# Slot tables of a routed MLP: single-pass products, shares behind the indices, bounds read in portions, a router on raw rows

## The reference, cut to what matters

```python
x = x + _L1_xattn_ref(_layernorm(x), ctx, ctx)      # gelu(xn @ ctx.T) @ ctx
xn = _layernorm(x)
logits = xn @ w_router                               # 8 experts
probs = softmax(logits); sel = argmax(probs); wgt = probs[sel]
for e in range(8):
    h = relu(xn @ w1[e] + b1[e]);  y = h @ w2[e] + b2[e]
    out = out + ((sel == e) * wgt)[:, None] * y
x = x + out
```

## Time and profile before

| | |
|---|---|
| median of 3 runs | 681.23 us (680.93 to 682.4) |
| the profiled execution: time | 682.95 us |
| its span | 681.0 us |
| TensorE busy | 583.7 us (86%) |
| VectorE busy | 494.2 us (73%) |
| ScalarE busy | 315.0 us (46%) |
| GpSimd busy | 271.3 us (40%) |
| `context_mlp`, from its first VectorE instruction to the meeting | 425.9 to 504.2 us |
| `experts` | 504.2 us to the end |

### The profile page before, as it was taken

One profiled execution on the slowest core, in us unless ns is written; L12 is line 12 of the kernel. 1 busy time (PEld: TensorE's weight loads), 2 busy tenths in 40 slices (PEclk: granted clock), 3 DMA queues, 4 the chain that ended last, 5 costly groups with the idle time before them and its releaser, 6 DMA issues. The chain is left out here.

```text
span 681.0 us, 11778 instructions
## 1 busy us (share of the span) xinstructions
PE 583.7 (86%) x3680; PEld 510.6 (75%) x3680; DVE 494.2 (73%) x961; ACT 315.0 (46%) x570; POOL 271.3 (40%) x270
## 2 busy tenths in 40 slices
PE   4489999995899999999999987678539799989983
PEld 3478988884688888888888876447528799879873
DVE  4799999984139888888988967476525866885682
ACT  1135545543258778778788850333101513442240
POOL 3434444660024344344354422032035652682341
PEclk9789999997899999999999999775558999989988
DMA  7122421100522322332232000814033441691100
GB/s 232 31 78 78 107 81 31 32 1 1 135 48 47 88 52 49 72 68 48 56 85 48 1 1 0 325 63 127 37 100 140 138 148 31 209 336 42 39 19 2
DMA packets 24123, 54.89 MB, mean 81 GB/s; under 512 B 4857, under 2 KB 9722, under 8 KB 22025
## 3 DMA queue, kind: packets, MB, share of 16 engines
q1 hardware_dynamic: 20328, 46.69, 23.2%
q0 software_dynamic: 2256, 5.54, 3.0%
q10 hardware_dynamic: 1488, 2.05, 1.0%
HBM read 33.27 MB, written 4.87 MB: 56 GB/s over the span
## 5 line engine op out<-in xcount | busy, mean ns | idle before, releaser
L939 POOL TENSOR_SCALAR h_p<-h_p,h_rs 128x1024 f32<-128x1024 f32 x64 | 72.2, 1128 | 116.3 <-DVE h_rs L1042 116.2
L1049 DVE TENSOR_REDUCE h_nmx<-h_psS 128x1 f32<-128x1024 f32 x64 | 78.2, 1221 | 28.7 <-PE h_psS L1141 27.4
L1029 DVE TENSOR_TENSOR h_pTl<-h_psT,h_pTh 128x512 fp32r<-128x512 f32 x128 | 81.6, 679 | 4.4 <-ACT h_pTh L969 4.4
L969 ACT CAST h_pTh<-h_psT 128x512 fp32r<-128x512 f32 x128 | 69.2, 590 | 31.3 <-PE h_psT L1099 31.2
L996 ACT ACTIVATE h_p<-h_psS,h_nmx 128x1024 f32<-128x1024 f32 x64 | 72.2, 1129 | 14.1 <-DVE h_nmx L1049 14.1
L1110 PE MATMUL h_psO<-h_pTh,h_vs 128*128 128x256 f32 x256 | 70.0, 306 | 3.0 <-DVE h_oT L1037 2.3
L1099 PE MATMUL h_psT<-ident,h_p 128*128 128x128 f32 x512 | 67.5, 273 | 1.4 <-DVE h_pTl L1029 1.2
L1099 PEld LDWEIGHTS h_psT<-ident,h_p 128*128 128x128 f32 x512 | 59.2, 140 | 11.2 <-issue 3.3
L341 POOL TENSOR_TENSOR a_p<-a_p,a_rs 128x616 f32<-128x616 f32 x32 | 39.0, 1219 | 62.8 <-DVE a_rs L445 62.7
L1110 PE MATMUL h_psO<-h_pTl,h_vs 128*128 128x256 f32 x256 | 63.6, 282 | 0.0
L1141 PE MATMUL h_psS<-h_kh,h_qs 128*128 128x512 f32 x128 | 55.7, 435 | 0.0
(11 more groups left out here) (295 smaller groups left out, 1498.5 us busy)
## 6 DMA issues: line engine op xcount, KB each, us to landing
wst<-in_m_w SPq DMA_DIRECT2D x16, 1024.0 KB, 5.8
bias<-in_m_b SPq DMA_DIRECT2D x8, 640.0 KB, 7.5
h_kh<-h_hi SPq DMA_DIRECT2D x30, 128.0 KB, 2.3
h_kl<-h_lo SPq DMA_DIRECT2D x30, 128.0 KB, 2.3
fw<-in_f_w SPq DMA_DIRECT2D x8, 384.0 KB, 4.1
rows<-x_all SPq DMA_DIRECT2D x4, 516.0 KB, 3.6
a_qs<-a_qhi SPq DMA_DIRECT2D x16, 128.0 KB, 2.3
a_qs<-a_qlo SPq DMA_DIRECT2D x16, 128.0 KB, 2.4
```

Source lines behind the costliest of these rows:

```text
L939: pool.tensor_scalar(pr[:, u % 4], pr[:, u % 4], rs[:, u:u + 1], 0.0, ALU.mult, ALU.add).then_inc(pn_ready, 1)
L969: act.copy(pTh[u // QP % 2][:, hf * HK:(hf + 1) * HK, u % QP * P:(u % QP + 1) * P], psT[hf][:]).then_inc(pT_hi, 1)
L1029: vec.tensor_tensor(pTl[u // QP % 2][part], psT[hf][:], pTh[u // QP % 2][part], ALU.subtract).then_inc(pT_lo, 1)
L1049: vec.tensor_reduce(nmx[:, u:u + 1], psS[u % 2][:], AX.X, ALU.max, negate=True).then_inc(max_ready, 1)
```

## The change: what it does

Four edits, all in `context_mlp` and `experts`.

- **Router on raw rows.** `normalise(NC + n)` is gone. TensorE transposes the rows of `x_all` as they are (waiting for `x_done`), and `route` multiplies them with `wrc`, the router's weights less their column means. The column sums come from a product with a matrix of ones (two products of 8 columns, placed behind `hidden(1)`), and VectorE makes `wrc` between `gelu(0)` and `normalise(2)`. The logits so lack the factor `rstd`, which VectorE multiplies into `e` after the subtraction of the largest.
- **Slots first, shares later.** `sent` has the token number alone, in fp32r, as `here` is; `inverse` is 16 products with 26 columns. The sum, the reciprocal, and a split of `wgt` in two parts, `whole` (fp32r) and `rest`, follow behind `here`. When `src` is written, VectorE makes `shared` (both parts, 52 columns), TensorE multiplies it with `here` (16 products), and VectorE adds the two results into `share`, last in the block.
- **Moved work.** The two `low_second` of expert 0 go from VectorE's stream in `context_mlp` to its `change(0)` in `experts`. The two `low_first` of expert 1 go from GpSimd's stream in `experts` to `context_mlp`, ahead of its wait for `src`. Gather 1 goes behind the meeting, and each tile is handed on three gathers later.
- **Bounds in portions.** The eight ends are read in portions of 2 to 4 between the first pieces of `change(0)` and `body(0, 0)`.

```diff
-        here = sb("c_here", [P, T, P])
-        sent = sb("c_sent", [P, T, 2, TG])
+        here = sb("c_here", [P, T, P], F32R)
+        sent, shared = sb("c_sent", [P, T, TG], F32R), sb("c_shared", [P, T, 2, TG], F32R)
+        whole, rest = sb("c_whole", [P, T], F32R), sb("c_rest", [P, T])
...
@@ gpsimd of context_mlp
             power(2)
             power(3)
+            for hf in range(2):
+                low_first(pool, t, 1, hf)
             pool.wait_ge(stored, 16 * NC)
             pool.wait_ge(src_ready, 1)
             gather(pool, t, 0)
-            gather(pool, t, 1)
...
@@ vector of context_mlp
             gelu(0)
+            vec.wait_ge(col_ps, 1)
+            vec.scalar_tensor_tensor(wrc[:], column.unsqueeze(1).to_broadcast([P, KD, NE]), -1.0 / D, wr[:], ALU.mult,
+                                     ALU.add).then_inc(wrc_ready, 1)
             normalise(2)
...
-                normalise(NC + n)
...
-            vec.tensor_tensor(e[:], psR[:], most, ALU.subtract).then_inc(shifted, 1)
+            link(vec.tensor_tensor(e[:], psR[:], most, ALU.subtract))
+            vec.wait_ge(rstd_ready, NC)
+            vec.tensor_tensor(e[:], e[:], rstd4.unsqueeze(2).to_broadcast(full), ALU.mult).then_inc(shifted, 1)
...
-            vec.wait_ge(exp_done, 1)
-            link(vec.tensor_reduce(tot[:], e[:], AX.X, ALU.add))
-            vec.reciprocal(wgt[:], tot[:])
...
-            for x, value in enumerate((tok1, wgt)):
-                ins = vec.tensor_tensor(sent[:, :, x], passed[:], value[:].unsqueeze(2).to_broadcast(wide), ALU.mult)
-            ins.then_inc(sent_ready, 1)
+            vec.tensor_tensor(sent[:], passed[:], tok1[:].unsqueeze(2).to_broadcast(wide), ALU.mult).then_inc(sent_ready, 1)
             for n in range(NC):
                 part, box = slice(n * CH, (n + 1) * CH), [P, CH, P]
                 vec.tensor_tensor(here[:, part], num[:].unsqueeze(1).to_broadcast(box),
                                   place[:, part].unsqueeze(2).to_broadcast(box), ALU.is_equal).then_inc(here_ready, 1)
-
-            for x in range(2):
-                low_second(vec, t, 0, x)
+            vec.wait_ge(exp_done, 1)
+            link(vec.tensor_reduce(tot[:], e[:], AX.X, ALU.add))
+            link(vec.reciprocal(wgt[:], tot[:]))
+            link(vec.tensor_copy(whole[:], wgt[:]))
+            link(vec.tensor_tensor(rest[:], wgt[:], whole[:].bitcast(F32), ALU.subtract))
 
             vec.wait_ge(inv_ps, 1)
...
+            vec.tensor_scalar(src[:], inverse, -1.0, 0.0, ALU.add, ALU.max).then_inc(src_ready, 1)
+            vec.tensor_tensor(shared[:, :, 0], passed[:], whole[:].bitcast(F32).unsqueeze(2).to_broadcast(wide), ALU.mult)
+            vec.tensor_tensor(shared[:, :, 1], passed[:], rest[:].unsqueeze(2).to_broadcast(wide),
+                              ALU.mult).then_inc(shared_ready, 1)
...
+            vec.wait_ge(share_ps, 1)
+            link(vec.tensor_copy(share[:], shares_in[:, 0]))
+            vec.tensor_tensor(share[:], share[:], shares_in[:, 1], ALU.add)
...
@@ tensor of context_mlp
+            pe.wait_ge(full_ready, 1)
+            for k in range(KD):
+                ins = pe.matmul(column, full_ones[:], wr[:, k], start=(k == 0), stop=(k == KD - 1))
+            ins.then_inc(col_ps, 1)
...
             ins.then_inc(inv_ps, 1)
+            pe.wait_ge(shared_ready, 1)
+            pe.wait_ge(dst_read, 1)
+            for i in range(T):
+                ins = pe.matmul(shares_in, here[:, i], shared[:, i], start=(i == 0), stop=(i == T - 1))
+            ins.then_inc(share_ps, 1)
...
@@ experts, tiles
-            ends = [load(eng, ENDS + e, MT - (NE - 1 - e), e + 2) for e in range(NE)]
-            change(0)
-            body(0, 0)
+            ends = []
+
+            def bounds(n):
+                for e in range(len(ends), len(ends) + n):
+                    ends.append(load(eng, ENDS + e, MT - (NE - 1 - e), e + 2))
+
+            change(0, bounds)
+            body(0, 0, bounds)
...
@@ gpsimd of experts
+            gather(pool, t, 1)
             gather(pool, t, 2)
-            arrived(pool, t, 0)
-            gather(pool, t, 3)
-            arrived(pool, t, 1)
-            gather(pool, t, 4)
-            arrived(pool, t, 2)
-            for hf in range(2):
-                low_first(pool, t, 1, hf)
-            for g in range(5, NG):
+            for g in range(3, NG):
+                arrived(pool, t, g - 3)
                 gather(pool, t, g)
-                arrived(pool, t, g - 2)
+            arrived(pool, t, NG - 3)
```

More of the change, by code:

```diff
@@ L1440, in transpose @@
             def transpose(i):
-                pe.wait_ge(xn_ready, i + 1)
+                n = i % NC
+                if i < NC:
+                    pe.wait_ge(xn_ready, i + 1)
+                else:
+                    pe.wait_ge(x_done, n + 1)
                 if i >= 1:
@@ L1615, in x_high, with change @@
                 act.copy(xh[:], psX[:]).then_inc(xh_ready, 1)
-            def change(e):
+            def change(e, bounds=None):
                 if e == 0:
@@ L1625, in change, with body @@
                         high_first(act, t, e + 1, hf)
-            def body(g, e):
+            def body(g, e, bounds=None):
+                if bounds:
+                    bounds(3)
                 x_high(g + 1)
+                if bounds:
+                    bounds(2)
                 for hf in range(2):
@@ L1657, in finish, with change @@
                                          ALU.add).then_inc(y_done, 1)
-            def change(e):
+            def change(e, bounds=None):
                 if e == 0:
+                    for x in range(2):
+                        low_second(vec, t, 0, x)
                     normalise(0)
@@ L1686, in body @@
                 normalise(g + 2)
+                if bounds:
+                    bounds(4)
             tiles(vec, change, body)
```

38 lines of the change are left out of this document (20 added, 18 removed).

## The result

| | before | changed |
|---|---|---|
| median | 681.15 us (680.93 to 682.4, 4 runs) | 672.56 us (667.16 to 673.38, 4 runs) |
| ratio, 95% interval | | 0.9855 [0.9824, 0.9885] |
| profiled execution: time, span | 682.95, 681.0 us | 673.38, 671.3 us |
| mean granted clock of that execution | 0.916 | 0.925 |

The change takes 8.6 us off the medians and 9.6 off the profiled executions. The forecast was a gain of 7.3 us and a median of 673.9.

A forecast was written before the change was run, and what follows sets the result against it. Four pieces in series were taken to bound the kernel: MLP's tail, slot stage, meeting, eight bound loads. 0.8 + 1.0 + 3.5 + 0.3 + 2.5 - 0.8 = 7.3 us gained gave 673.9 us, range 670.2 to 678.2.

The forecast's parts named there:

- (a): Router on raw rows, MLP's tail: earlier update and output product, less the column sums' delay; net 0.8 us gained.
- the 1.6 us that I named as the upper end: MLP's tail: extra gain if the earlier start kept or regained full clock for output product and transposes; not counted on.
- (b): Slot tables: sum, reciprocal and second multiply leave the chain ahead of the token product; 1.0 us gained.
- (c): Token product: 16 passes with 26 columns instead of 32 with 52, at 0.22 us each; 3.5 us gained.
- Rival 1: Narrow single passes run near the bf16 pace, so both slot products get shorter; 671.5 us, chance 0.16.
- (d): From `src` to the meeting: VectorE's wait for the shares replaces GpSimd's drain as last; 0.3 us gained.
- (e): Start of the experts: two `low_second` replace eight loads ahead of VectorE's first normalise; 2.5 us gained.
- (f): First tiles: remaining bound loads cost 0.3 us and a shifted clock rise 0.5; together 0.8 us lost.
- The experts are taken to shift as a whole: Behind the first tiles: the experts keep their length, since TensorE fills them; forecast gain there 0.
- Rival 2: First tiles: gather 1, issued late beside `low_second`, holds up the first bias add; 3.3 us lost, 677.2 us, chance 0.13.
- Rivals 3 and 4: Single narrow passes cost as much as two, 680.9 us, chance 0.04; experts' tiles at half clock, 684.5 us, chance 0.05.

The follow-up runs named there:

- two_pass: The changed kernel with one-hots, tokens and shares back in plain f32, two passes a product; 679.21 us, ratio 0.9978.
- warm_slots: The changed kernel with wide TensorE products, results unread, as clock fillers in the slot stage and at the experts' start; 671.12 us, ratio 0.9862.
- bf16: The changed kernel with one-hots in bf16 instead of fp32r, token number and share each as two bf16 parts; 672.16 us, ratio 0.9846.
- bounds_first: The changed kernel with all eight bounds read first again on every engine; 678.88 us, ratio 0.996.
- the repeat: The changed kernel run once more with no edit, in another batch; 674.73 us, ratio 0.9881.
- low_second_back: The changed kernel with both `low_second` of expert 0 back ahead of VectorE's wait for the token product; 672.25 us, ratio 0.9854.
- gaps: The changed kernel with one `low_second` of expert 0 ahead of VectorE's wait for the tokens, one ahead of that for the shares; 671.77 us, ratio 0.9877.
- combined: The changed kernel with bf16 one-hots, both `low_second` behind the shares but ahead of the meeting, TensorE's bounds as 2, 2, 4; 676.94 us (with fillers 677.27).
- router_only: The kernel before the change with only the router's edits; 680.84 us, ratio 0.9988.
- warm_router: As warm_slots, with more fillers there and others in the MLP's tail and router, against the changed kernel; 669.36 us, ratio 0.9807.

## Why the prediction was right, point by point

(a) Gained 1.33, forecast 0.8. The delay of the column sums is as forecast: the first update comes 9.81 us behind the first gelu instead of 9.36, 0.45. The term was too small at the output product: it started 1.05 us earlier by stages, and ran at full clock for its first 0.3 us (to 461.9), so that its eight passes took 3.47 us instead of 3.75. That is worth the other 0.3, a small piece of the 1.6 us that I named as the upper end; the tail itself stayed at 0.50.

(b) Gained 0.94, forecast 1.0.

(c) Gained 3.4, forecast 3.5. The open question, whether a single narrow pass costs one of the two, is answered by 3.56 us for 16 passes and by 7.00 for two_pass. Of the two bounds the one from the load records held: the passes start 0.213 us apart at half clock, and in warm_slots 0.112 apart at full clock, within each group of four. The rule of the Trainium skill (TensorE: Matmul & The Clock Gate, section "LDWEIGHTS (loading the stationary operand)"), a load of 107 ns for 128 columns, is near the spacing at full clock and half of that at half clock. bf16 came at 0.027 at half clock. Rival 1 was right that such a pace moves the bound elsewhere, and too hopeful on GpSimd's drain.

(d) Gained 0.1, forecast 0.3: VectorE is last, 5.8 us behind `src`. Of the 5.5 us that I had added up, the shares' product starts 1.64 us behind `src` instead of 1.5 and VectorE's copy 3.62 behind its start; the drain and the meeting behind the last add take 0.3 more.

(e) Gained 2.6, forecast 2.5. bounds_first (5.4 us lost) shows that the portions carry it.

(f) Lost 0.7, forecast 0.8, by the clock and not by the loads: of the twelve first hidden products those from the second to the last start 0.43 us apart (504.65 to 508.91), where before they came faster from the tenth on (515.44, the next at 515.67). The first tile's bias adds waited for TensorE as before; VectorE's four late loads stood hidden behind output products.

**Where it was off.** "The experts are taken to shift as a whole" failed in the profiled pair: from the second tile on another 3 us were gained. Two places carry it. At the change to the second expert TensorE waits 2.45 us for `wl` instead of 3.63:

```profile
526.42 2.35 DVE L1820 TENSOR_TENSOR wl<-wst,wh 128x1024 fp32r<-128x1024 f32 x2
526.60 1.95 POOL L1826 DMA_INDIRECT xg<-rows,src  x1 [0.31 <-issue]
528.57 4.77 POOL L1606 TENSOR_TENSOR wl<-wst,wh 128x1024 fp32r<-128x1024 f32 x2
...
533.68 0.79 PE L1746 MATMUL e_psH<-wh,e_xh 128*128 128x512 f32 x1 [2.45 <-POOL wl L1606]
```

Before, the gather beside `low_second` took 3.09 us and the split began 3.12 us behind it; here it took 1.95 and the split begins 1.97 behind. This is a matter of alignment, not of work saved: five kernels built on the change have a gather of 3.08 us again, somewhere in the experts. At the last change of expert the clock decides. Windows of 7 us around it, in the changed kernel and, in the second fence, before:

```profile
648.00:655.00 7.00, 4.56 (x28) 3.74 (x26) 6.82 (x9) 3.17 (x5) 3.33 (x3) 1.00 0.02 7
```

```profile
656.00:663.00 7.00, 4.60 (x16) 3.54 (x14) 6.82 (x8) 2.96 (x4) 3.53 (x3) 0.76 0.02 7
```

TensorE's wait is the same (2.44 and 2.40 us); before, the clock fell behind it, and the last two stores gained 1.5 us here that they gained in no other expert. Neither belongs to the change for certain: the clock fell at this place in five kernels built on the change, and before ran between 677.21 and 683.0 us in one batch, with its profiled execution at 682.95. By the medians the gain is 8.6 us, and 7.0 in the repeat (681.74 less 674.73), on either side of the 7.3 forecast, so the profiled pair flatters the change, and part of what it gained behind the second tile is luck.

Rival 2 did not happen in this kernel, and not for the reason I gave. I looked at GpSimd's issue beside `low_second`, which took 1.37 us, not 3.09. What protects gather 1 is that `low_second`, standing behind the meeting, holds SP's fetches back until 501.99. I had noted that delay as harmless to expert 2; that it is a benefit to gather 1 only the four kernels without it showed. Its price is not one number: 0.3 us to the second tile in low_second_back and gaps, 5.2 in combined. Rivals 3 and 4 are excluded by the 3.56 us of 16 passes, beside the 7.00 of two_pass, and by the clock of 1.00 from 509.6 on.

Left open: why GpSimd's drain lasts 3.4 to 3.6 us in nine profiles and 4.2 to 4.4 in five (before, router_only, two_pass, warm_slots, bf16), so that it ended 5.4 us behind `src` in bf16 and 4.4 in the change; why a late gather 1 cost so much more in combined; and what the clock did in the execution of 667.16 us, of which there is no trace.

## What to carry to other kernels

A product with few columns costs its passes: in f32 and fp32r 26 columns took as long as 52. Choose the type by the number of passes and by what one pass costs (0.213 us in fp32r, 0.027 in bf16, at half clock). Before moving a piece out of one cover into another, look at whom it signals: here the step that cost 2.4 us on VectorE also held back the fetches behind which gather 1 lands 3.4 to 4.6 us later, which cost 5 us in the combined kernel. And an edit that saves a microsecond alone can lose it to a collision that another part of the change removes (router_only).

## What the runs showed of the hardware that I had not expected

- VectorE's 0.41 us normalise took 2.58 us beside a GpSimd subtract that began 0.10 us later (router_only), and a VectorE operation of 0.29 us took 1.71 beside one that had begun 0.8 us earlier (warm_router).
- At half clock narrow fp32r passes start 0.213 us apart with 26 columns and with 52, bf16 ones 0.027 with 26 and 0.043 with 52.
- An indirect gather issued 0.8 us behind the weight fetches landed 6.6 to 7.8 us after its issue (four kernels), and 3.2 us after it when it went ahead of them (issued at 500.33).
- 12 us of transposes and 8-column products, TensorE busy 11.5 to 12.0 of 12 us, stayed at 0.50; with one 512-column product for every four of the 8-column ones, behind rows of them that had brought the clock up, the same stretch ran at 1.00 (warm_router).
- The time of one kernel moves by some 3 us either way from execution to execution (677.21 to 683.0 before, in one batch), with granted clocks of 0.916 to 0.940 over the profiles.
